# Node rows of the second gate added from 128-row parts by 32-row products, a pair of tiles at a time, and two more tiles that take their queries from TensorE

## What is computed

```python
def _gate(h, q, Wg, bg, Wq, bq):
    B, L, F = q.shape                                   # 8, 64, 768
    N = h.shape[0] // B                                 # 8 nodes of a graph
    h3 = h.reshape(B, N, F)
    hg = jnp.einsum('bnf,gf->bng', h3, Wg[:, :F])       # one row for each node
    qg = jnp.einsum('blf,gf->blg', q, Wg[:, F:]) + bg   # one row for each query
    attn = jax.nn.sigmoid(hg[:, :, None, :] + qg[:, None, :, :])
    qi = jnp.einsum('bnlf,blf->bnf', attn, q)
    alpha = jax.nn.sigmoid(jnp.einsum('bnf,gf->bng', h3, Wq[:, :F]) + jnp.einsum('bnf,gf->bng', qi, Wq[:, F:]) + bq)
    hn = alpha * jnp.tanh(qi) + (1.0 - alpha) * h3
    return hn.reshape(B * N, F)
```

## Time and profile before

| what | value |
|---|---|
| median of 3 runs | 287.77 us (287.75 to 288.59) |
| the profiled execution's own time | 286.82 us |
| its span in the profile | 284.9 us |
| mean granted clock of TensorE | 0.986 |
| the second gate in that span | from about 149.6 to 193.8 us |

### The profile page before, as it was taken

The page is one execution under the profiler, slowest core; times in us unless marked ns, Lnnn a source line. Parts: engine busy times, 40 slices in busy tenths (PEclk is TensorE's granted clock), DMA queues, the critical chain, the costliest instruction groups (busy, mean ns, idle before and its releaser), DMA issues.

```text
span 284.9 us, 3987 instructions
## 1 busy us (share of the span) xinstructions
PE 263.1 (92%) x1605; PEld 122.7 (43%) x1605; DVE 145.5 (51%) x252; ACT 93.4 (33%) x155; POOL 93.6 (33%) x80
## 2 busy tenths in 40 slices
PE   7999999999899989999996899999989979998994
PEld 7764854455345522344332223223434343433441
DVE  0835540019999998430148797983541135114512
ACT  2412420035759976020025656741200041003000
POOL 7480000004999998000035888950000000000000
PEclk9999999999999999999999999999999995999999
DMA  7999995992009856006999500000897090000001
GB/s 243 369 401 401 402 351 175 408 403 91 0 0 329 337 167 171 0 2 238 404 403 401 215 0 2 0 0 2 319 402 276 0 330 3 0 0 2 1 2 28
DMA packets 21028, 51.84 MB, mean 182 GB/s; under 512 B 4105, under 2 KB 4361, under 8 KB 21010
## 3 DMA queue, kind: packets, MB, share of 16 engines
q1 hardware_dynamic: 20400, 51.35, 48.7%
q10 hardware_dynamic: 610, 0.24, 0.4%
HBM read 51.39 MB, written 0.20 MB: 181 GB/s over the span
## 4 chain that ended last, share of the span: by engine, by line
PE 65%; DVE 16%; POOL 9%; issue 7%; ACT 2%; DVEq 0%; POOLq 0%; ACTq 0%
PE ps L913 26%; POOL prod L527 9%; PE ps L1204 6%; PE ps L990 6%; PE ps L887 4%; DVE prod L773 3%; PE ps L965 3%; DVE pre L787 3%; PE ps L1104 3%; PE ps L1078 3%; PE ps L1049 2%; PE ps L971 2%; DVE stack L759 2%; PE ps L1270 2%; PE ps L949 1%
## 5 line engine op out<-in xcount | busy, mean ns | idle before, releaser
L527 POOL TENSOR_TENSOR prod<-pre,qn 128x768 f32<-128x768 f32 x38 | 74.0, 1969 | 11.4 <-ACT pre L603 9.0
L787 DVE TENSOR_TENSOR pre<-ps,qg 128x768 f32<-128x768 f32 x49 | 45.6, 950 | 8.0 <-PE ps L1078 7.3
L603 ACT ACTIVATE pre<-pre 128x768 f32<-128x768 f32 x49 | 41.2, 847 | 18.8 <-DVE pre L787 17.9
L913 PE MATMUL ps<-W,nodeT 128*64 128x384 f32 x216 | 39.8, 504 | 0.0
L913 PE MATMUL ps<-W,prod 128*64 128x384 f32 x240 | 39.5, 487 | 0.0
L1078 PE MATMUL ps<-stack,bsel 96*128 96x384 bf16 x128 | 31.5, 329 | 5.2 <-DVE pre L787 2.8
L990 PE MATMUL ps<-W 128*128 128x384 f32 x96 | 34.7, 490 | 0.9 <-DVE W L389 0.7
L389 ACT COPY W<-ps 128x384 f32<-128x384 f32 x40 | 18.2, 482 | 40.1 <-PE ps L887 40.0
L1104 PE MATMUL ps<-prod,rsel 128*32 128x384 f32 x256 | 27.3, 497 | 3.1 <-POOL prod L527 2.2
L517 POOL COPY stack<-hi 32x384 bf16<-32x384 bf16 x4 | 2.2, 555 | 78.3 <-DVE hi L751 78.1
L913 PEld LDWEIGHTS ps<-W,prod 128*64 128x64 f32 x240 | 16.6, 137 | 21.1 <-issue 20.2
(11 more groups left out here) (174 smaller groups left out, 230.2 us busy)
## 6 DMA issues: line engine op xcount, KB each, us to landing
W<-in_L_gnn_W SPq DMA_DIRECT2D x9, 2304.0 KB, 10.4
W<-in_L_gnn_W_rel SPq DMA_DIRECT2D x6, 2304.0 KB, 16.2
W<-in_L_gnn_Wg SPq DMA_DIRECT2D x4, 1152.0 KB, 11.9
W<-in_L_gnn_W_root SPq DMA_DIRECT2D x2, 2304.0 KB, 9.8
W<-in_L_gnn_Wq SPq DMA_DIRECT2D x4, 1152.0 KB, 8.0
qn<-in_L_gnn_query_embs SPq DMA_DIRECT2D x4, 384.0 KB, 11.1
xa<-in_x ACTq DMA_DIRECT2D x2, 96.0 KB, 7.5
out<-t SPq DMA_DIRECT2D x2, 96.0 KB, 2.2
```

What stands on the lines that cost most here:

```text
L527: nc.gpsimd.tensor_tensor(prod[:, T % PRODS, :], pre_of(T), qn[:, pair_and_node(t)[0], :], ALU.mult).then_inc(prod_p, 1)
L603: nc.scalar.activation(dst, src, ACT.Sigmoid).then_inc(sig_ready, 1)
L787: nc.vector.tensor_tensor(dst, ring(T), by_half(qg[:, pair_and_node(t)[0], :]), ALU.add).then_inc(pre_ready, 1)
L913: ins = nc.tensor.matmul(ps[c * N:(c + 1) * N, bank, 0:HD], T[:, j, col0 + h * N:col0 + (h + 1) * N], w[:, k, c * HD:(c + 1) * HD], start= ...
```

## The change

It does four things, all for the second gate (layer 1) except for the size of two constants.

1. The stack is no longer filled. VectorE makes the low part with one subtraction of 128 x 384 into a new tile `low`; ScalarE's and POOL's eight copies and VectorE's four subtractions of 32 rows go.
2. The products are made for a pair of tiles together (`add_pair`): for each of the three parts, four products with 32 rows of contraction: tile g of the pair and column half c take the rows c*64 + g*32 to + 32 of the part. So 12 products of 32 x 128 with 384 columns take the place of 4 of 96 x 128. The four of one part read four different row quarters and write four different banks.
3. Before a pair, TensorE waits for the slots of both of its tiles, and makes the copies of both if they are D; the pair's products follow behind.
4. Kinds: tiles 13, 25 and 29 become D, tile 27 becomes X (all were the other one before), so D or T are 8 tiles where they were 6, and X are 7 where they were 9.

The constants `bsel` and `i3` grow from 96 to 128 rows (`i4`); the first gate and the biases use their first 96 rows.

```diff
         KINDS = ["P" if t in POOL_TILES else "V" for t in range(TILES)] + list(
-            "TD" "PX" "PX" "PP" "PD" "PX" "PX" "PP" "PX" "PD" "PX" "PP" "PX" "PD" "PX" "XD")
+            "TD" "PX" "PX" "PP" "PD" "PX" "PD" "PP" "PX" "PD" "PX" "PP" "PD" "PX" "PD" "XD")
...
-            for g in range(3):
-                rows = i3[g * GN:(g + 1) * GN, :]
+            for g in range(P // GN):
+                rows = i4[g * GN:(g + 1) * GN, :]
...
                 for i, (part, ready, stacked) in enumerate(((hi, hi_ready, hi_stacked), (mid, mid_ready, mid_stacked))):
+                    if layer == 1:
+                        break
...
-                for g in range(2):
-                    for h in range(2):
-                        stack_low(g, h)
+                if layer == 0:
+                    for g in range(2):
+                        for h in range(2):
+                            stack_low(g, h)
+                else:
+                    nc.vector.tensor_tensor(low[:, :], t1[:, :], mid[:, :], ALU.subtract).then_inc(low_ready, 1)
...
+            def add_pair(T):
+
+                t = T - TILES
+                for part, ready in ((hi, hi_ready), (mid, mid_ready), (low, low_ready)):
+                    if t == 0:
+                        pe.wait_ge(ready, 1 if part is low else 2)
+                    for g in range(2):
+                        for c in range(2):
+                            rows = slice(c * N + g * GN, c * N + (g + 1) * GN)
+                            ins = nc.tensor.matmul(ring(T + g)[:, c, :], bsel[rows, t // 2, :], part[rows, :],
+                                                   start=(part is hi and KINDS[T + g] not in TENSOR_ADD),
+                                                   stop=(part is low))
+                        if part is low:
+                            ins.then_inc(hg_cast, 1)
...
-                        for c in range(2):
-                            if KINDS[T] in TENSOR_ADD and T not in AHEAD:
-                                copy_queries(T, c)
-                            ins = nc.tensor.matmul(ring(T)[:, c, :], bsel[:, t // 2, :],
-                                                   stack[:, c, t % 2, :], start=KINDS[T] not in TENSOR_ADD, stop=True)
+                        for c in range(2):
+                            ins = nc.tensor.matmul(ring(T)[:, c, :], bsel[0:3 * GN, t // 2, :],
+                                                   stack[:, c, t % 2, :], start=True, stop=True)
                         ins.then_inc(hg_cast, 1)
+                    if layer == 1 and t < TILES and t % 2 == 0:
+                        for g in range(2):
+                            wait_ring_free(T + g)
+                            if KINDS[T + g] in TENSOR_ADD and T + g not in AHEAD:
+                                for c in range(2):
+                                    copy_queries(T + g, c)
+                        add_pair(T)
```

More of the change, by code:

```diff
@@ L73, in gnn_kernel @@
         avg = sb("avg", [P, P])
-        bsel = sb("bsel", [3 * GN, PPG * NB, P], BF16)
-        i3 = sb("i3", [3 * GN, GN], BF16)
+        bsel = sb("bsel", [P, PPG * NB, P], BF16)
+        i4 = sb("i4", [P, GN], BF16)
+        i3 = i4[0:3 * GN, :]
         rsel = sb("rsel", [P, N])
@@ L85, in gnn_kernel @@
         mid = sb("mid", [P, HD], BF16)
+        low = sb("low", [P, HD], BF16)
         M = sb("M", [P, R * N])
@@ L190, in gnn_kernel @@
         mid_ready = sem("mid_ready")
+        low_ready = sem("low_ready")
         hi_stacked = [sem(f"hi_stacked_{g}") for g in range(2)]
@@ L486, in _ @@
             link(nc.gpsimd.memset(rsel[L:P, GN - 1 + NB:GN + NB], 1.0))
-            link(nc.gpsimd.memset(i3[:, :], 0.0))
-            for g in range(3):
-                rows = i3[g * GN:(g + 1) * GN, :]
+            link(nc.gpsimd.memset(i4[:, :], 0.0))
+            for g in range(P // GN):
+                rows = i4[g * GN:(g + 1) * GN, :]
                 link(nc.gpsimd.affine_select(out=rows, in_=rows, compare_op=ALU.not_equal, fill=1.0, base=0,
@@ L492, in _ @@
             for g in range(PPG):
-                rows = i3[:, g * 2 * NB:(g + 1) * 2 * NB].rearrange("p (b n) -> p n b", b=2)
+                rows = i4[:, g * 2 * NB:(g + 1) * 2 * NB].rearrange("p (b n) -> p n b", b=2)
                 nc.gpsimd.tensor_copy(bsel[:, g * NB:(g + 1) * NB, :].rearrange("p n (b l) -> p n b l", b=2),
-                                      rows.unsqueeze(3).to_broadcast([3 * GN, NB, 2, L])).then_inc(consts_ready, 1)
+                                      rows.unsqueeze(3).to_broadcast([P, NB, 2, L])).then_inc(consts_ready, 1)
             nc.gpsimd.memset(qk[:, :, :, :], 0.0).then_inc(qk_cleared, 1)
@@ L964, in keep_warm @@
                 for _ in range(n):
-                    nc.tensor.matmul(ps[:, bank, :], bsel[:, 0, :], bsel[:, 0:4, :].rearrange("p a b -> p (a b)"),
+                    nc.tensor.matmul(ps[:, bank, :], bsel[0:3 * GN, 0, :], bsel[0:3 * GN, 0:4, :].rearrange("p a b -> p (a b)"),
                                      start=True, stop=True, skip_group_check=True)
@@ L1050, in copy_queries, with wait_ring_free @@
                                  start=True, stop=False)
+            def wait_ring_free(T):
+                before = before_in_ring(T)
+                if before is not None:
+                    if KINDS[before] in "XD":
+                        wait_multiplied(pe, before)
+                    elif KINDS[before] == "T":
+                        pe.wait_ge(sig_ready, before + 1)
+                    else:
+                        pe.wait_ge(pre_ready, vec_adds(before + 1))
+            def add_pair(T):
[11 more added lines that the diff above has]
+                            ins.then_inc(hg_cast, 1)
             def gate(layer):
@@ L1057, in gate @@
                     T = layer * TILES + t
[L1058 to L1061, removed]
+                    if layer == 0 and t < 2:
+                        pe.wait_ge(hi_stacked[t], 2)
+                        pe.wait_ge(mid_stacked[t], 2)
+                        pe.wait_ge(lo_stacked[t], 2)
                     if layer == 1 and t == TILES:
@@ L1065, in gate @@
                         keep_warm(1, TRA if layer == 0 else 2 * ring_slot(2 * TILES - 3))
[L1066 to L1074, removed]
+                    if layer == 0 and t < TILES:
+                        wait_ring_free(T)
                         for c in range(2):
-                            if KINDS[T] in TENSOR_ADD and T not in AHEAD:
-                                copy_queries(T, c)
-                            ins = nc.tensor.matmul(ring(T)[:, c, :], bsel[:, t // 2, :],
-                                                   stack[:, c, t % 2, :], start=KINDS[T] not in TENSOR_ADD, stop=True)
+                            ins = nc.tensor.matmul(ring(T)[:, c, :], bsel[0:3 * GN, t // 2, :],
+                                                   stack[:, c, t % 2, :], start=True, stop=True)
                         ins.then_inc(hg_cast, 1)
+                    if layer == 1 and t < TILES and t % 2 == 0:
[5 more added lines that the diff above has]
+                        add_pair(T)
                     if layer == 1 and t < 2:
```

## The result

| | before | after |
|---|---|---|
| median | 287.99 us (4 runs) | 292.82 us (4 runs, 292.33 to 294.21) |
| profiled execution, its span | 286.82, 284.9 | 292.76, 290.9 |
| mean granted clock in it | 0.986 | 0.979 |

The medians differ by 4.8 us (1.7%). The ratio on record is 1.0228, with a 95% interval of 1.0163 to 1.0292; that is more than the two medians give, and the record doesn't show which executions of the kernel before went into it. By either the change is slower: its lowest execution, 292.33, lies 3.7 us above the highest of the kernel before, 288.59. The forecast was 293.7, in a range of 290.0 to 297.0.

A forecast was written before the change was run, and what follows sets the result against it. It took the second gate as bound by VectorE's and TensorE's order together, worst at D tiles. +6.96 in the gate, -0.25 at its end and -0.78 at its start gave +5.9: 287.77 to 293.7 us, range 290.0 to 297.0.

The forecast's parts named there:

- The walk: Second gate, add of one even tile to the next: 14 intervals from tile 2 to 30 sum to 43.80 us, +6.96.
- Part 1: Start of the second gate, without the stack: add of tile 2 at 151.26 instead of 152.04, a gain of 0.78 us.
- Part 2: Price of a pair's 12 products of 32 rows on TensorE: 0.79 us as an estimate, 0.54 from below.
- Two at a time: Rival: only two row quarters run together, a pair takes 1.17 us instead of 0.75, total 299.6 us; chance 0.07.
- no overlap: Rival: a pair's products run one at a time, 2.13 us instead of 0.75, total 313.0 us; chance 0.05.
- Part 3: D pairs: even tile's product stands behind the odd tile's wait and copies; multiply to add 3.22 us, without D 1.77.
- Part 4: Kinds: two fewer adds save 1.74 us of VectorE if it were the bound; instead two more pairs pay for the order.
- The sum: Whole kernel: +5.9 us at the gate's end; profiled execution 286.82 to 292.7 us, median 287.77 to 293.7 us.
- Signs: Profile after: VectorE idle about 1.5 us before adds of tiles 8, 12, 18, 24, 28, 30; add of 30 near 195.
- work decides: Rival: VectorE's total work, not order, sets the gate, which gets 2.5 us shorter, total 285.3 us; chance 0.11.

The follow-up runs named there:

- e1_warm: The changed kernel with filler products for TensorE in its three idle stretches ahead of pair 8; median 292.18 us, gate length 43.85 us.
- e4: The changed kernel with the copies of each D tile made twice; median 302.20 us, gate length 54.62 us.
- e2: The changed kernel, with the even tile's six products first in pairs whose odd tile is D; median 293.44 us, gate length 43.54 us.
- e7_no_d: The kernel of e1_warm with X in place of every D behind tile 1; median 284.98 us, ratio 0.9942 to the kernel before.
- e10: The changed kernel with the old kinds, even tile's products first in D pairs, and the fillers of e1_warm; median 288.43 us, ratio 1.0022 to the kernel before.
- e9: The changed kernel with fillers, behind tile 1 only tile 31 still D, its pair's even tile first; median 282.07 us, ratio 0.9832 to the kernel before.
- e11: The kernel before with X in place of D at tiles 9, 19 and 27; median 283.38 us, ratio 0.9860 to the kernel before.
- e3: The changed kernel with the kinds of the kernel before; median 290.25 us, gate length 43.49 us.
- e5: The kernel of e1_warm with a pair's 12 products ordered quarter by quarter; median 290.50 us against 292.18, gate length 43.98 us.

## Why the prediction held, point by point

**The walk.** It is a walk at full clock; the changed kernel itself took 46.45 with its fall. In e1_warm, where the clock is full, the intervals between the adds of even tiles were 2.67, 2.69, 4.16, 1.72, 4.13, 2.67, 2.67, 3.20, 2.67, 2.67, 4.15, 2.18, 4.13 and 4.14; forecast 2.64, 2.69, 4.11, 1.77, 4.09, 2.65, 2.65, 3.22, 2.65, 2.65, 4.10, 2.40, 4.09 and 4.09. Sum 43.85 against 43.80. The only one off by more than 0.1 is 24 to 26 (2.18 for 2.40). TensorE's queue sets it, as forecast, but I had added durations that include the way through the array (2.40 is 0.75 + 0.8 + 0.85), where the starts are apart by 0.59, 0.80 and 0.78 (186.16, 186.75, 187.55, 188.33 in TensorE's timeline of the changed kernel).

**Part 1.** The add of tile 2 came at 150.85 instead of 152.04. Of these 1.19 us, 0.30 were there before the change acts (`hi` is cast at 145.92, and was at 146.22; over all profiles of both families it lies between 145.87 and 146.35, so this is spread between executions), which leaves 0.89 for a forecast of 0.78. `low` took 0.56 and `mid` 0.36 instead of 0.71.

**Part 2.** From the start of a pair's products to the add that waits for it: 163.99 to 164.69, 0.70; forecast 0.75. Copies and change of shape: 166.66 to 168.12, 1.46; forecast 1.45. Two at a time and no overlap are both out. The Trainium skill (TensorE: Matmul & The Clock Gate, Measured speedup vs the span model) gives 3.07 times for four row tiles. The trace agrees that they run together; but it has 0.17 from one group of four to the next, 0.01 over a single product's 0.16, and the 0.79 that the prediction estimated from that page was too much by 0.09.

**Part 3, the large term.** Right in size and in mechanism: waits at pairs 8, 12, 18, 24, 28 and 30, and e4 shows all of them on the path. What it doesn't say is what another order would save. I put the wait on the order; from the add of tile 10 on, at full clock, e2 gives back only 3.0 of the 7.0 us between e1_warm (32.61) and e7_no_d (25.58). The rest goes only with the D tiles themselves: it is TensorE's own time at a D tile, for which the next pair then waits. And with the order in a D pair and the kinds both undone (e10), 2.5 us of the gate still stand against the kernel before. They go mostly with D tiles too (without any before tile 31, e9 and e11 differ by 0.6), but no run parts what the 32-row products and what the common wait of a pair have in them.

**Part 4.** Right in sign: the added D tiles cost 2.6 us of the median in e3 and 2.9 of the gate from tile 10 on, 3.4 by the walk.

**The sum.** That the profiled execution lost 5.9 us (292.76 against 286.82), just what was forecast, is partly luck. The walk is right by itself, but two terms that I didn't have nearly cancel: the clock in the gate (+2.6) and the kernel before's own fall behind it (-2.2). Sum of the profile: -0.3 ahead of the change, -0.9 at the start, +9.6 in the gate (of which 2.6 by the clock), and -0.25 from there to the gate's end give 8.2, and 6.0 remain at the end of the span. At full clock alone the loss is 5.8 to 6.1; the walk said 5.9. The medians moved by 4.8 only. The clock of the executions behind the 287.99 isn't on record, so where the other 1.1 us lie stays open. The prediction's sentence that what comes after the gate moves with it holds for the order of the work, not for its clock.

**Signs.** VectorE stood about 1.5 before the adds of tiles 12, 18, 24 and 28, as foretold, but 2.31 before that of tile 30, and 3.15 before that of tile 8, by the clock. The add of tile 30 came at 197.30 for 195, by the clock too.

**Rivals.** That work decides is out: VectorE was busy 141.9 us where it had been 145.5, and yet waited 18.5 us in the gate.

## What to carry to other kernels

When an engine's queue gains a wait, ask what stands behind it in the same queue: here a product that VectorE needed at once was put behind a wait and 1.4 us of copies that belonged to another tile. Moving an add of 0.87 us from a busy engine to another's f32 copies of 1.3 to 1.4 us pays only if that engine's queue has the room at that moment, not on average; inside this gate it had none, and without those tiles both kernels got faster. And walk such a ring before the change: a handful of prices from a few rows gave 14 intervals to within 0.05 us, but for one.

## What the hardware showed beyond that

- Products on different row quarters overtake each other: their order in the queue made no difference (e5: 43.98 against 43.85).
- Four products of 32 rows in four quarters and four banks take 0.17 us together, as one of 96 rows took 0.16.
- The clock gave and took more than the change's smaller terms: the same kernel took 284.2 at a mean granted clock of 0.998 and 288.6 at 0.970. With one fall taken away (e1_warm), another stands behind the gate in the profiled execution, and by their mean clock two of the other three have one as well, for no gain in the median that can be told. Why it falls in the third layer in some executions and not in others stays open.
- What a fall costs depends on what stands in it: 2.6 us in the changed kernel's gate, nothing in e11's. So two executions with the same mean clock can differ: the kernel before took 286.33 at 0.980 and 288.24 at 0.981.
